# Replicating q in one pass over halves exchanged by DMA, and row 0's outer products on one engine, in a gated-linear-attention layer with a feed-forward block

## The reference, cut to what matters

```
q, k, v = x @ Wq, x @ Wk, x @ Wv          # as 16 heads of 8 channels
gate = exp(log_sigmoid(x @ Wgk1 @ Wgk2 + bgk2) / 16)
state = state * gate[..., None] + v[..., None] * k[..., None, :]   # a scan over the tokens
out_t = einsum('bhvk,bhk->bhv', state, q_t)
out   = layernorm(out) * silu(x @ Wg) @ Wout
x     = layernorm(x + out)
h     = silu((x @ w1) * s1) * ((x @ w2) * s2)
h     = gelu((h @ h1) * s3);  h = gelu((h @ h2) * s4)
x     = layernorm(x + (h @ w3) * s5)
```

## Time and profile before

| what | value |
|---|---|
| median of 3 timed runs | 180.81 us (180.43 to 182.13) |
| the profiled execution's own time | 180.24 us |
| its span, first to last instruction | 178.4 us |
| PE / PE weight loads busy | 91% / 69% of the span |
| DVE / ACT / POOL busy | 80% / 62% / 64% |
| granted PE clock, mean | 0.998 of full |

### The profile page before, as it was taken

How to read it: one execution, slowest core, us unless ns; L and a number is a source line. 1 busy time by engine, 2 the same in 40 slices (tenths; PEclk the granted TensorE clock), 3 DMA queues, 4 the chain that set the end, 5 groups by cost and what they waited for, 6 DMA issues and landing times.

```text
span 178.4 us, 2680 instructions
## 1 busy us (share of the span) xinstructions
PE 162.1 (91%) x802; PEld 123.3 (69%) x802; DVE 142.0 (80%) x304; ACT 111.1 (62%) x179; POOL 114.9 (64%) x98
## 2 busy tenths in 40 slices
PE   0897989999889999999999999999999999999980
PEld 0765757768658786877778768578776875887870
DVE  0499989968798996698999987989998895864062
ACT  4554779993237736287683427667946288996731
POOL 8997898959807689972377998708685330705032
PEclk9999999999999999999999999999999999999999
DMA  3999920000000000000000000000010000031202
GB/s 105 297 387 416 396 70 0 0 4 0 4 0 0 0 2 0 4 2 0 0 0 0 0 0 0 0 0 0 4 59 0 0 2 0 4 85 48 61 4 63
DMA packets 6495, 8.97 MB, mean 50 GB/s; under 512 B 561, under 2 KB 5202, under 8 KB 5970
## 3 DMA queue, kind: packets, MB, share of 16 engines
q1 hardware_dynamic: 5906, 5.93, 10.5%
q0 software_dynamic: 576, 2.88, 4.2%
HBM read 7.76 MB, written 1.05 MB: 49 GB/s over the span
## 4 chain that ended last, share of the span: by engine, by line
PE 47%; DVE 12%; ACT 5%; issue 4%; POOL 2%; DVEq 0%; POOLq 0%
PE ffn L608 9%; PE ffn L617 8%; PE att L530 6%; PE att L514 3%; PE att L515 3%; PE ffn L586 3%; DVE f_lo L1173 3%; PE ffn L591 2%; PE att L655 2%; PE ffn L674 2%; PE att L643 2%; PE ffn L667 2%; ACT f_hi L894 2%; PE att L541 2%; DVE full L1162 1%
## 5 line engine op out<-in xcount | busy, mean ns | idle before, releaser
L1074 DVE TENSOR_TENSOR_SCAN state<-gate,att 128x512 f32<-128x512 f32 x32 | 38.3, 1208 | 1.9 <-PE att L530 1.9
L367 POOL TENSOR_TENSOR f_lo<-full,f_hi 128x512 fp32r<-128x512 f32 x18 | 23.0, 1291 | 25.1 <-DVE full L1162 18.1
L894 ACT ACTIVATE f_hi<-ffn,vec_cols 128x512 fp32r<-128x512 f32 x24 | 16.5, 687 | 27.4 <-PE ffn L617 27.0
L326 POOL TENSOR_TENSOR u_tok<-kv_tok 128x1024 f32<-128x1024 f32 x14 | 30.8, 2208 | 0.6 <-DVE o_acc L1094 0.5
L608 PE MATMUL ffn<-f_hi,h_hi 128*128 128x512 f32 x96 | 28.1, 408 | 0.2
L617 PE MATMUL ffn<-f_lo,h_hi 128*128 128x512 f32 x96 | 26.1, 399 | 0.0
L341 POOL TENSOR_TENSOR o_acc<-o_acc,y 128x512 f32<-128x512 f32 x16 | 20.6, 1290 | 7.7 <-DVE y L1086 7.5
L608 PEld LDWEIGHTS ffn<-f_hi,h_hi 128*128 128x128 f32 x96 | 17.6, 189 | 6.0 <-ACT f_hi L894 1.5
L617 PEld LDWEIGHTS ffn<-f_lo,h_hi 128*128 128x128 f32 x96 | 17.9, 189 | 4.1
L530 PE MATMUL att<-ident,u_tok 128*128 128x128 f32 x128 | 18.5, 275 | 1.3 <-DVE u_tok L1051 0.9
L530 PEld LDWEIGHTS att<-ident,u_tok 128*128 128x128 f32 x128 | 15.0, 141 | 5.5 <-DVE u_tok L1051 1.3
(11 more groups left out here) (177 smaller groups left out, 347.0 us busy)
## 6 DMA issues: line engine op xcount, KB each, us to landing
h_raw<-in_hT SPq DMA_DIRECT2D x2, 1024.0 KB, 12.2
h_hi<-in_hT POOLq DMA_DIRECT2D x2, 1024.0 KB, 12.0
x_tok<-in_x SPq DMA_DIRECT2D x4, 256.0 KB, 5.4
out<-out_tok SPq DMA_DIRECT2D x3, 256.0 KB, 2.3
w_raw<-in_w12T SPq DMA_DIRECT2D x1, 512.0 KB, 5.0
w_hi<-in_w12T POOLq DMA_DIRECT2D x1, 512.0 KB, 8.7
xT_raw<-in_xT SPq DMA_DIRECT2D x1, 256.0 KB, 2.7
proj_raw<-in_proj SPq DMA_DIRECT2D x2, 128.0 KB, 2.4
```

The source lines that it names most:

```text
L326: nc.gpsimd.tensor_tensor(u_tok[:, j].rearrange("p k (h v) -> p k h v", v=DH), v_b.unsqueeze(1).to_broadcast([P, DH, HEADS, DH]), k_b.unsq ...
L367: nc.gpsimd.tensor_tensor(lo[:, o], full_block(layer, o), hi[:, o].bitcast(F32), ALU.subtract).then_inc(pool_rested, 1)
L894: nc.scalar.activation(hidden[layer][0][:, o], bank[:], ACT.Gelu, scale=scales[:, 1 + layer, o:o + 1]).then_inc(gelu_hi_ready, 1)
L1074: nc.vector.tensor_tensor_scan(state[:, k % 3], gate[:, b], A[2 + k % 2][:], 0.0, ALU.mult, ALU.add).then_inc(scanned, 1)
```

## The change

- q's channels are permuted on the host (`Wq`'s columns), so that the channels k = 0 to 3 of all heads lie on partitions 0 to 63 and k = 4 to 7 on partitions 64 to 127. `rep` has four column sets instead of eight, each with its ones in both halves of the partitions. `rep_f` is half as large; it is filled by two affine selects, the second waiting for the first.
- Row 0: the two passes of a round stay, but run over the 64 partitions of the round's half.
- Rows 1 to 3: after `q_lo_ready`, SP sends q_hi's upper half and q_lo's lower half to a buffer in DRAM and back, exchanged (`q_swap`). `q_hi` then holds both parts of channels k < 4, `q_lo` both parts of k >= 4, and one pass over 128 partitions replicates the sum. Round 0 of row 1 waits for the exchange of row 1; round 0 of rows 2 and 3 for those of rows 2 and 3.
- Row 0's four outer products are all made by DVE, none by POOL.

```diff
--- before.py
+++ after.py
@@ -20,6 +20,7 @@
     DH = HID // HEADS
     TILES = L // P
     OB = D_HID // P
+    HALF = P // 2
     assert HID == P and L == 512 and DH == 8 and OB == 4
 
     with ExitStack() as ctx:
@@ -44,7 +45,7 @@
             "place_out", B * ROW, ("w12_raw", [P, 2, D_HID], F32, 0), ("w3_raw", [P, OB, HID], F32, 2 * ROW),
             ("out_tok", [P, B, TILES, HID], F32, 0))
         rep_f, xT0_raw, y = arena(
-            "place_y", 4 * ROW, ("rep_f", [P, DH, P], F32, 0), ("xT0_raw", [P, L], F32, 3 * ROW), ("y", [P, 4, L], F32, 0))
+            "place_y", 4 * ROW, ("rep_f", [P, DH // 2, P], F32, 0), ("xT0_raw", [P, L], F32, 3 * ROW), ("y", [P, 4, L], F32, 0))
         x_tok = sb("x_tok", [P, B, TILES, HID])
         proj_raw = sb("proj_raw", [P, 4, HID])
         proj_hi = sb("proj_hi", [P, 5, HID], F32R)
@@ -68,7 +69,7 @@
         w3_lo = sb("w3_lo", [P, OB, HID], F32R)
         ident = sb("ident", [P, P])
         center = sb("center", [P, P])
-        rep = sb("rep", [P, DH, P], F32R)
+        rep = sb("rep", [P, DH // 2, P], F32R)
         lo_sums = sb("lo_sums", [P, 6])
         lo_any = sb("lo_any", [P, 6])
         lo_flag = sb("lo_flag", [1, 1], mybir.dt.int32)
@@ -78,6 +79,7 @@
         kv_tok = sb("kv_tok", [P, B, TILES, 2 * HID])
         q_hi = sb("q_hi", [P, B, L], F32R)
         q_lo = sb("q_lo", [P, B, L], F32R)
+        q_swap = nc.dram_tensor("q_swap", [2, B - 1, HALF, L], F32).ap()
         silu_g = sb("silu_g", [P, B, L])
         z_a, x2_hi, x2_lo = arena(
             "place_x2", 2 * ROW, ("z_a", [P, 2, L], F32, 0), ("x2_hi", [P, L], F32R, 0), ("x2_lo", [P, L], F32R, ROW))
@@ -123,7 +125,10 @@
         w3_loaded = sem("w3_loaded")
         consts_zero = sem("consts_zero")
         consts_ready = sem("consts_ready")
+        rep_half = sem("rep_half")
         rep_ready = sem("rep_ready")
+        q_swap_out = sem("q_swap_out")
+        q_stacked = [sem(f"q_stacked{b}") for b in range(1, B)]
         ones_row_ready = sem("ones_row_ready")
         proj_hi_ready = sem("proj_hi_ready")
         proj_lo_ready = sem("proj_lo_ready")
@@ -254,7 +259,6 @@
         KV_BANKS = ((A[1], A[2]), (F[3], F[2]), (F[3], F[2]), (F[3], F[2]))
         Q_BANK = (A[0], F[0], F[0], A[1])
         G_BANK = (F[1], F[0], F[2], F[3])
-        U_ON_DVE = (2, 3)
         block = ctx.enter_context(nc.Block())
 
         @block.sync
@@ -275,6 +279,13 @@
             sp.dma_start(h_raw[:, 1], hT[:, 1]).then_inc(h2_loaded, 16)
             sp.dma_start(w3_raw[:], w3T).then_inc(w3_loaded, 16)
             sp.dma_start(x_tok[:, 0], x_rows[0]).then_inc(x_loaded[0], 16)
+            for b in range(1, B):
+                sp.wait_ge(q_lo_ready, b + 1)
+                sp.dma_start(q_swap[0, b - 1], q_hi[HALF:P, b].bitcast(F32)).then_inc(q_swap_out, 16)
+                sp.dma_start(q_swap[1, b - 1], q_lo[0:HALF, b].bitcast(F32)).then_inc(q_swap_out, 16)
+                sp.wait_ge(q_swap_out, 32 * b)
+                sp.dma_start(q_hi[HALF:P, b].bitcast(F32), q_swap[1, b - 1]).then_inc(q_stacked[b - 1], 16)
+                sp.dma_start(q_lo[0:HALF, b].bitcast(F32), q_swap[0, b - 1]).then_inc(q_stacked[b - 1], 16)
 
             def store_out(b):
                 sp.wait_ge(out_ready, TILES * (b + 1) + 1)
@@ -305,7 +316,11 @@
             pool.wait_ge(consts_zero, 2)
             rep_v = rep_f[:].rearrange("p k (h v) -> p k h v", v=DH)
             nc.gpsimd.affine_select(out=rep_v, in_=rep_v, compare_op=ALU.not_equal, fill=1.0, base=0,
-                                    pattern=[[-1, DH], [-DH, HEADS], [0, DH]],
+                                    pattern=[[-1, DH // 2], [-(DH // 2), HEADS], [0, DH]],
+                                    channel_multiplier=1).then_inc(rep_half, 1)
+            pool.wait_ge(rep_half, 1)
+            nc.gpsimd.affine_select(out=rep_v, in_=rep_v, compare_op=ALU.not_equal, fill=1.0, base=-HALF,
+                                    pattern=[[-1, DH // 2], [-(DH // 2), HEADS], [0, DH]],
                                     channel_multiplier=1).then_inc(consts_ready, 1)
             nc.gpsimd.memset(half_neg[:], -0.5).then_inc(consts_ready, 1)
             nc.gpsimd.memset(eps[:], EPS).then_inc(consts_ready, 1)
@@ -398,7 +413,6 @@
             pool.dma_start(h_hi[:, 0], hT[:, 0]).then_inc(h1_hi_loaded, 16)
             pool.dma_start(h_hi[:, 1], hT[:, 1]).then_inc(h2_hi_loaded, 16)
             pool.dma_start(w3_hi[:], w3T).then_inc(w3_hi_loaded, 16)
-            outer_products(0, [j for j in range(TILES) if j not in U_ON_DVE])
             weight_lo(0)
             weight_lo(1)
             sum_over_k(0, (1,))
@@ -503,6 +517,8 @@
                         pe.wait_ge(q_lo_ready, 1)
                     else:
                         pe.wait_ge(x2_lo_ready, b)
+                        for stacked in (q_stacked[0:1] if isinstance(b, int) else q_stacked[1:]):
+                            pe.wait_ge(stacked, 32)
                 elif k == 1:
                     if isinstance(b, int) and b == 0:
                         pe.wait_ge(kv_copied, 1)
@@ -511,8 +527,15 @@
                         pe.wait_ge(e_sum_ready, b)
                 else:
                     pe.wait_ge(y_ready, DH * b + k - 1)
-                nc.tensor.matmul(q_bank(b, k)[:], rep[:, k], q_hi[:, b], start=True, stop=False)
-                nc.tensor.matmul(q_bank(b, k)[:], rep[:, k], q_lo[:, b], start=False, stop=True).then_inc(q_rep_ready, 1)
+                half, n = k // (DH // 2), k % (DH // 2)
+                if isinstance(b, int) and b == 0:
+                    part = slice(half * HALF, (half + 1) * HALF)
+                    nc.tensor.matmul(q_bank(b, k)[:], rep[part, n], q_hi[part, b], start=True, stop=False)
+                    nc.tensor.matmul(q_bank(b, k)[:], rep[part, n], q_lo[part, b], start=False,
+                                     stop=True).then_inc(q_rep_ready, 1)
+                else:
+                    nc.tensor.matmul(q_bank(b, k)[:], rep[:, n], (q_hi, q_lo)[half][:, b], start=True,
+                                     stop=True).then_inc(q_rep_ready, 1)
 
             def transpose_u(b, k):
                 if k == 0:
@@ -1257,8 +1280,8 @@
             dve.wait_ge(proj_hi_ready, 3)
             nc.vector.tensor_tensor(proj_lo[:, 2:4], proj_raw[:, 2:4], proj_hi[:, 2:4].bitcast(F32),
                                     ALU.subtract).then_inc(proj_lo_ready, 1)
-            outer_product(0, U_ON_DVE[0])
-            outer_product(0, U_ON_DVE[1])
+            for j in range(TILES):
+                outer_product(0, j)
             log_gate(0)
             rest_of_q(0)
             rest_of_x(1)
@@ -1359,7 +1382,8 @@
     D_HID, HID = get["ffn_w1_w"].shape
     OB = D_HID // HID
     x = get["attn_x"]
-    proj = np.stack([get[f"attn_{n}"] for n in ("Wk", "Wv", "Wq", "Wg")], axis=1)
+    channels = np.arange(HID).reshape(16, 2, HID // 32).transpose(1, 0, 2).reshape(HID)
+    proj = np.stack([get["attn_Wk"], get["attn_Wv"], get["attn_Wq"][:, channels], get["attn_Wg"]], axis=1)
     cols = [get[f"ffn_{n}"].reshape(OB, HID) for n in ("w1_s", "w2_s", "h1_s", "h2_s")]
     cols += [get[n].reshape(1, HID) for n in ("ffn_w3_s", "attn_gamma", "attn_beta")]
     hT = [get[f"ffn_{n}"].T.reshape(OB, HID, D_HID) for n in ("h1_w", "h2_w")]
```

## The result

The changed kernel takes 179.39 us in the median of four runs (178.72 to 180.29); the kernel before, beside it on the same chip, 181.47 (180.43 to 182.13). The ratio is 0.9889, with a 95% interval of 0.984 to 0.9938: 1.1% faster. The forecast was 179.2, in a range of 178.1 to 180.6. Its time came true; of its steps some were too large and others too small, as the traces show. The profiled execution took 179.29 us with a span of 177.5 (first to last instruction), against 180.24 and 178.4 before: 0.9 us less, where the forecast had 1.56.

The account below looks back on a forecast made before the run. VectorE was taken to bound rows 1 to 3, TensorE keeping nearly equal pace. 1.25 (first scan) - 0.4 (boundaries) + 0.71 (rows 1 to 3) = 1.56 us off 180.24: 178.7, median 179.2; range 178.1 to 180.6, own range 178.4 to 180.2.

Parts of the forecast that it names:

- What bounds the kernel: From round 3 to the last sum VectorE works without a gap; most of TensorE's 24 removed passes (5.6 us) bring nothing.
- the rival of 174.3: TensorE is the bound, so all 24 passes count: 6.5 us off, 174.3; chance 5%.
- Products: Row 0: four outer products on VectorE at about 1.1 us each bring gate and first scan about 0.95 us earlier.
- the rival of 184.1: Row 0's products stay at 2.57 us each on VectorE without POOL; 3.3 us slower, 184.1; chance 7%.
- Constants: Row 0: clearing half as much lets POOL come earlier, x's rest 0.3 us earlier (bounds 0 and 0.38).
- Boundaries: Row 0: each change between 64 and 128 partitions costs TensorE 0.19 us, about ten of them, 0.4 on the path.
- the second rival: Row 0: each boundary drains TensorE for 0.37 us, half on the path; only 0.71 gain stays, 180.1; chance 15%.
- Rows 1 to 3: One replication pass instead of two brings `center_o` earlier by 0.27, 0.22 and 0.22 us in rows 1, 2, 3: 0.71.
- The forecast of 33.4: Sign in the changed profile: distance between the rows at 33.4 us instead of 33.63.
- Exchange: q's transfers through DRAM for row 1 take some 6 us, done at about 40, before its first replication; cost 0.
- The sum: 1.25 - 0.4 + 0.71 = 1.56 us off the profiled 180.24, giving 178.7; 179.2 for the median.
- a clock too unlikely to be a case: TensorE's granted clock falls from 2.4 GHz because it now waits; would show as passes 0.43 apart instead of 0.23.

Follow-up runs that it names:

- three passes: The changed kernel with the replications of rounds 0 to 6 in rows 1 to 3 sent three times; ratio 0.9987 to the kernel before.
- products back: The changed kernel with row 0's outer products of tiles 0 and 1 on POOL again, 2 and 3 on VectorE; ratio 0.9971 to the kernel before.
- products alone: The kernel before with only row 0's four outer products all on VectorE; 179.43 us against 181.86, ratio 0.9886.
- full width: The changed kernel with row 0's replications on all 128 partitions, none on 64; 179.40 us, ratio 0.987 to the kernel before.
- the version with the early bias pass: The changed kernel with row 0's first gate bias pass sent earlier, small product in another bank, POOL's row 2 normalisation before w_tok's multiplication; 179.14 us, ratio 0.9868.
- the kernel with added work: The changed kernel with seven identity products added on TensorE around the first small product; ratio 0.9896 to the kernel before.

## Why the prediction was right, point by point

**What bounds the kernel.** Right. VectorE's loop sets the time of rows 1 to 3. 24 passes less, the exchange, the constants and the 64-partition form give 0.14 to 0.16 us at `og` without the products, and doubling the passes of rounds 0 to 6 costs 0.02. The rival of 174.3, with TensorE as the bound, is excluded: with three passes, 9.7 us more work cost 1.97.

**Products.** Right in place and size. The forecast had 0.95 with the gate at 13.1; products back measured 0.93, and the gate is at 13.30 behind Ln. Without POOL beside them the products follow one another every 1.14 us (four in 4.63), near the 1.08 read from the stretch behind POOL's end, and the rival of 184.1 is excluded. How much of the lead is kept to the end depends on TensorE's pace in row 0: 0.96 us between products back and the changed kernel's first profile, 0.7 in products alone. The Trainium skill (VectorE: DVE Perf Modes, the section on the errata) gives a formula by which such a lone product would be estimated at 1.22 us; the trace agrees, with records of 1.22 us each that overlap by 0.08.

**Constants.** Wrong in size: forecast 0.3, measured 0.12 (x's rest ends at 5.11 for 5.23). What counts is when POOL ends, for x's rest ends 0.46 to 0.47 behind it in every profile. POOL's two selects:

```profile
2.33 1.08 POOL L318 TENSOR_SCALAR_AFFINE_SELECT rep_f<-rep_f 128x512 f32<-128x512 f32 x1
3.56 1.09 POOL L322 TENSOR_SCALAR_AFFINE_SELECT rep_f<-rep_f 128x512 f32<-128x512 f32 x1
```

They end at 4.65, where the single one had ended at 4.76: 0.11 earlier, and so is x's rest. They begin 0.43 earlier, but together they take 2.32 with the gap between them, not 2.00: each takes 1.08, more than half, and the second begins 0.14 behind the first. I had put both too low; they take back three quarters of the shorter clearing.

**Boundaries.** Right as a mechanism, 0.36 to 0.37 us of issue out of 64 partitions and none of it at full width; too large on the path, 0.4 forecast and 0.13 measured. ScalarE's copy of q would have kept VectorE waiting by 0.30 without them, a cover that I had not named. The Trainium skill (TensorEngine Tiling (Array Packing), Key Properties) has changes of the tiling mode drain TensorE; the runs agree that something stands before each such load. At the price of the second rival, 0.37 each and half of it on the path, row 0 would have given back what it gained, which it did not.

**Rows 1 to 3.** The step that failed. Forecast 0.27 + 0.22 + 0.22 = 0.71; measured 0.22 + 0 + 0 (the load of `center` in row 1 stands 0.42 behind the sum for 0.64, the column for row 1 has 0.21, and the distances from row 1 to 2 and from 2 to 3 are 33.29 and 33.64 for 33.28 and 33.62). The term for rows 2 and 3 was a lateness of `center_o` read off the chain's start of 103.67, where TensorE's own timeline has the load at 103.45, 0.06 behind the sum. The forecast of 33.4 for the distance of the rows fell with it. Nor do rounds 3 to 6 wait for y nearly each: in every row only round 7's replication shows it, 0.27 to 0.29 us; besides, two transposes a row wait about 0.2 us each for the scan.

**Exchange.** Right: cost 0, and row 1's halves back at 38.7 (36.03 + 2.7) for the forecast of 40.

**The sum.** Forecast for the profile 1.56; the terms as measured are 1.04 for the first scan, less 0.13, plus 0.22, which is 1.13, and `og` of row 3 has 1.10. That profile had an early pace; the second one of the changed kernel, with a late one, has 0.74. The tail lost 0.5 of the first's to a transfer that was long by chance; the first output addition has 0.58 there. The median fell by 2.1 us, though, twice what the starts explain. The times of the kernel before fall into two groups: of its 64 timed executions that count, 27 took 179.94 to 180.94 us and 37 took 181.28 to 182.75, none between, and the profiled one, 180.24, is of the lower group. So its median depends on how many fall in which, 180.81 to 181.86 over the sets of runs. The 14 of the changed kernel, 178.72 to 180.29, have their median (179.39) beside their profiled executions (179.29, 179.26), 1.2 under the 180.57 of the lower group; products alone has 179.43. No execution of the upper group was profiled, so what makes it longer is open. That the time agrees with the forecast to 0.2 us is in part luck: the forecast took 1.56 off 180.81, and the profiled executions differ by 0.95. The low end of my own range was wrong too: by its terms, 1.56 + 0.4 + 0.08 = 2.04 off 180.81, it is 178.8 and not 178.4.

## What to carry to other kernels

Before counting a lateness, read it from the two engines' own timelines, end of the one and load of the other; the chain's starts are not starts of instructions, and one that is 0.2 us off in a loop counts once a row. Passes taken out of an engine whose results are never waited for are worth at most the one that stands between the last wait and the end of the stage. A gain at the head of a program is kept only as far as the next engine's lead reaches: 0.54 us gained in the middle of row 0 became 0.13 at its end. And before two profiles are compared, the stretch ahead of the edit must be seen to be alike in both: here one kernel differs from itself by 0.38 us at the end of row 0.

## What the runs showed that I had not expected

In 13 of 14 profiles TensorE runs its first passes, until 12.8 us at least, at 1.2 GHz, passes of 512 columns 0.43 us apart, and in one it changed at about 8.7. The prediction had the 0.43 as a mark of a clock too unlikely to be a case; it was there in the kernel before. The moment differs between executions of one kernel. The transposes of row 0's first two rounds (128 columns each), in the changed kernel's first and second profile and in the version with the early bias pass:

```profile
13.24 1.47 PE L553 MATMUL att<-ident,u_tok 128*128 128x128 f32 x8
```

```profile
13.24 1.91 PE L553 MATMUL att<-ident,u_tok 128*128 128x128 f32 x8
```

```profile
12.82 1.85 PE L552 MATMUL att<-ident,u_tok 128*128 128x128 f32 x8
```

They stand 0.21 us apart before the change of pace and 0.11 behind it; it came at 13.7, about 14.9 and about 14.5, and the first two last sums of row 0 are at 34.59 and 34.97. With all the products on VectorE these transposes lie at 13.2 to 14.7, in the very stretch in which the pace changes; with two on POOL they come at 14.4 and find it done. TensorE had been busy without a gap from 5.69 us on in the changed kernel, and in the kernel with added work from 1.95 on, where the pace changed no earlier (13.8).

A transfer of 64 KB, w_row, lands in 2.5 or in 4.5 us in the same kernel, behind the same two transfers. A wait of POOL for such a load, ahead of work that others need, makes a half microsecond of scatter in the end.
